# The row maxima brought to the queries by matrix products and copies instead of transfers

## The reference, cut to what matters

```python
# self (units 0 to 15)
scores = where(tril == 0, NEG, where(key_mask == 0, NEG, relu(x@Wq+bq) @ relu(x@Wk+bk).T / sqrt(8)))
out = softmax(scores) * query_mask @ relu(x@Wv+bv) + x ; x = LN(x + gamma * norm(out) + beta)
# ctx (units 16 to 31): 64 rows of another sequence are the keys and values
x = LN(x + softmax(q @ k.T) @ v)
# ffn (units 32 to 47), then experts chosen for each token: the two best of 8
x = x + softmax(causal(q @ k.T)) @ v @ wo + bo
x = x + sum over the 2 best experts of  gate * ffn_e(LN(x))
# ffn (units 48 to 63), then experts chosen for each sequence; LN at the end
```

## Time and profile before

| | us |
|---|---|
| median of 3 runs | 1480.73 (1480.18 to 1484.06) |
| the profiled execution's own time | 1489.51 |
| its span, first to last instruction | 1487.7 |
| PE, DVE, ACT, POOL busy | 1226.8, 949.5, 721.2, 667.1 |
| idle of PE before L714 and L706 until a transfer of the maxima | 54.5 and 10.5 |

### The profile page before, as it was taken

The page is one execution under the profiler, slowest core; times in us unless marked ns, Lnnn a source line. Parts: engine busy times, 40 slices in busy tenths (PEclk is TensorE's granted clock), DMA queues, the critical chain, the costliest instruction groups (busy, mean ns, idle before and its releaser), DMA issues. The chain is left out here.

```text
span 1487.7 us, 29555 instructions
## 1 busy us (share of the span) xinstructions
PE 1226.8 (82%) x9414; PEld 980.7 (66%) x9414; DVE 949.5 (64%) x2854; ACT 721.2 (48%) x1527; POOL 667.1 (45%) x1151
## 2 busy tenths in 40 slices
PE   0598889998898679999997299993788989967998
PEld 0476667775665457777776289982566666746997
DVE  6478799997667688888873201112788787623554
ACT  0165566664444346555653155551355555544543
POOL 2244445464222137777776200003576676432655
PEclk9899999997658789999997589996699999987999
DMA  2676776433555445454521277873555555305774
GB/s 49 178 202 197 207 206 182 118 88 112 149 152 154 127 119 135 127 141 122 135 76 35 61 203 216 222 198 86 159 144 148 138 138 142 99 27 163 204 222 141
DMA packets 210607, 212.86 MB, mean 143 GB/s; under 512 B 46868, under 2 KB 163092, under 8 KB 210453
## 3 DMA queue, kind: packets, MB, share of 16 engines
q1 hardware_dynamic: 193572, 189.59, 47.4%
q10 hardware_dynamic: 12784, 12.98, 2.8%
q0 software_dynamic: 4096, 8.40, 2.0%
HBM read 121.84 MB, written 84.41 MB: 139 GB/s over the span
## 5 line engine op out<-in xcount | busy, mean ns | idle before, releaser
L1215 POOL TENSOR_SCALAR_AFFINE_SELECT probs<-probs 128x256 f32<-128x256 f32 (+1 forms) x576 | 282.1, 495 | 266.2 <-ACT probs L901 261.0
L901 ACT ACTIVATE probs<-weights 128x512 f32<-128x512 f32 x448 | 264.5, 597 | 180.9 <-PE weights L714 142.1
L1061 DVE TENSOR_REDUCE negmax<-scores 128x4 f32<-128x512 f32 x384 | 260.5, 685 | 81.3 <-PE scores L667 78.7
L714 PE MATMUL weights<-queries,keys 104*128 104x256 f32 x768 | 170.5, 307 | 55.0 <-DMA queries<-maxrows 54.5
L714 PEld LDWEIGHTS weights<-queries,keys 104*128 104x128 f32 x768 | 145.5, 205 | 89.6 <-DMA queries<-maxrows 70.5
L667 PE MATMUL scores<-keys,queries 128*128 128x512 f32 (+1 forms) x384 | 192.3, 507 | 8.0 <-DMA queries<-zeros 3.7
L901 ACT ACTIVATE probs<-weights,keybias 128x512 f32<-128x512 f32 x192 | 131.6, 688 | 96.6 <-PE weights L714 77.3
L1065 DVE TENSOR_REDUCE negmax<-scores 128x2 f32<-128x512 f32 (+1 forms) x192 | 129.6, 684 | 42.0 <-PE scores L673 35.1
L1279 POOL DMA_INDIRECT out_room<-expert_rows,y_index x64 | 63.6, 994 | 193.4 <-POOLq L1528 180.8
L719 PEld LDWEIGHTS weights<-queries,keys 104*128 104x128 f32 x768 | 113.9, 196 | 16.5 <-ACT probs L901 6.3
L719 PE MATMUL weights<-queries,keys 104*128 104x128 f32 x768 | 111.4, 269 | 5.0 <-ACT probs L901 4.8
(11 more groups left out here) (257 smaller groups left out, 2662.7 us busy)
## 6 DMA issues: line engine op xcount, KB each, us to landing
windows<-parts SPq DMA_DIRECT2D x192, 192.0 KB
queries<-windows SPq DMA_DIRECT2D x64, 384.0 KB
keys<-windows SPq DMA_DIRECT2D x192, 96.0 KB
hidden_room<-in_m_w SPq DMA_DIRECT2D x71, 256.0 KB, 2.8
out_room<-in_m_w SPq DMA_DIRECT2D x71, 256.0 KB, 3.1
routed_rows<-zeros SPq DMA_DIRECT2D x64, 256.0 KB, 3.2
windows<-parts ACTq DMA_DIRECT2D x64, 120.0 KB
xin<-routed_rows SPq DMA_DIRECT2D x39, 128.0 KB, 3.0
```

What stands on the lines that cost most here:

```text
L714: i = pe.matmul(bank[:, k * T:(k + 1) * T], keys[0:MREND, S4 * a + s, 0:P], queries[0:MREND, s, :], start=True, stop=True)
L901: act.activation(probs[:, n % RING], weight_banks[n % 2][:], ACT.Exp, scale=SCALE, **bias).then_inc(exp_done.sem, 1)
L1061: i = dve.tensor_reduce(most[:, part, s, :], bank[:].rearrange("p (a k) -> p a k", k=P), AX.X, ALU.max, negate=True)
L1215: pool.affine_select(out=block, in_=block, compare_op=ALU.is_ge, fill=0.0, base=0, pattern=[[0, heads], [1, P]], channel_multiplier=-1).th ...
```

## The change

- **Maxima.** `maxparts` keeps its 32 columns at the right end (96 to 127) and zeros ahead of them. A product with the 104 columns from `8*s` on as the stationary side then puts the 8 rows of group s at rows 96 to 103 of the bank. `pe_maxima` does that for two groups in one slot (four products of 128 columns, a full bank) and for the other two in the next. `act_maxima` copies rows 96 to 103 straight into `queries`, one copy of 8 by 512 for each half. The second half's products wait for the first half's copy, and `pe_values_in` for the second's. `maxrows` and `sp_maxrows` are gone.
- **Masks.** `keybias`, `keep` and `keeps` are made by POOL (`pool_masks`), and so is `offset` (`pool_offset`); DVE waits for both.
- **Hiding.** The twelve transfers begin at slot 30, one every 11 or 12 slots.
- **Routing.** `earlier`, `ones` and `route_mask` have the type float32r, that of the kernel's score products, and the two products with `earlier` become one of 16 columns.

```diff
@@ pe_maxima
-            bank.take(pe)
-            for t in range(NT):
-                i = pe.matmul(X[:, t * P:(t + 1) * P], maxparts[g % 2][:, t, :], ident_r[:], start=True, stop=True)
-            i.then_inc(maxT_ready.sem, 1)
-            bank.until(maxrows_taken.sem, maxrows_taken.at(g))
-            yield
+            for half in range(2):
+                bank.take(pe)
+                for k in range(2):
+                    s = 2 * half + k
+                    for t in range(NT):
+                        i = pe.matmul(X[0:MREND, k * T + t * P:k * T + (t + 1) * P], maxparts[g % 2][:, t, 8 * s:8 * s + MREND],
+                                      ident_r[:], start=True, stop=True)
+                i.then_inc(maxT_ready.sem, 1)
+                bank.until(maxrows_placed.sem, maxrows_placed.at(g, half + 1))
+                yield
@@ pe_attend
-            pe.wait_ge(maxrows_placed.sem(g), maxrows_placed.at(g))
+            pe.wait_ge(maxrows_placed.sem, maxrows_placed.at(g, NT))
@@ act_maxima
-            act.wait_ge(maxT_ready.sem, maxT_ready.at(g))
-            if g >= 2:
-                act.wait_ge(maxrows_placed.sem(g - 2), maxrows_placed.at(g - 2))
-            act.copy(M8[g % 2][:], maxima_bank(g).tensor[0:S4 * 8, 0:T]).then_inc(maxrows_taken.sem, 1)
-            yield
+            X = maxima_bank(g).tensor
+            act.wait_ge(stacked.sem(g), stacked.at(g))
+            for half in range(2):
+                act.wait_ge(maxT_ready.sem, maxT_ready.at(g, half + 1))
+                act.copy(Q[g % LANES][MROW:MREND, 2 * half:2 * half + 2, :],
+                         X[MROW:MREND, :].rearrange("p (s t) -> p s t", s=2)).then_inc(maxrows_placed.sem, 1)
+                yield
@@ sp_hiding
-            yield from rest(60)
+            yield from rest(30)
...
+                    yield from rest(11)
...
-                    yield from rest(3)
+                    yield from rest(11)
@@ pe_route
-            pe.matmul(X[:, 0:E], earlier[:], mask[:, 0], start=True, stop=True)
-            pe.matmul(X[:, E:2 * E], earlier[:], mask[:, 1], start=True, stop=False)
-            pe.matmul(X[:, E:2 * E], ones[:], mask[:, 0], start=False, stop=True)
+            pe.matmul(X[:, 0:2 * E], earlier[:], mask[:].rearrange("p t e -> p (t e)"), start=True, stop=True)
+            pe.matmul(X[:, E:2 * E], ones[:], mask[:, 0], start=False, stop=True, skip_group_check=True)
@@ new, on POOL at slots prepare+1 and outputs+3 of a self unit
+        def pool_masks(pool, g):
...
+            pool.wait_ge(gone_ready.sem, gone_ready.at(g))
...
+            pool.tensor_scalar(keybias[:, seq], gone[:], -BIG, None, ALU.mult)
+            pool.tensor_scalar(keep2[g % 2][:], gone[:, :, None].to_broadcast([P, NT, 2]), -1.0, 1.0, ALU.mult, ALU.add)
+            pool.tensor_scalar(keeps[:, seq], gone[:], -1.0, 1.0, ALU.mult, ALU.add).then_inc(masks_ready.sem, 1)
+        def pool_offset(pool, g):
+            pool.wait_ge(resid_loaded.sem(g), resid_loaded.at(g))
...
+            pool.tensor_tensor(offset[:], resid[g % LANES][:], w["a_beta"][:, None, :].to_broadcast([P, NT, C]),
+                               ALU.add).then_inc(offset_ready.sem, 1)
```

54 lines of the change are left out of this document (26 added, 28 removed).

## The result

| kernel | median us (lowest to highest, runs) | ratio to before, 95% interval |
|---|---|---|
| before | 1482.39 (1480.18 to 1485.59, 4) | |
| after | 1443.34 (1437.15 to 1445.59, 4) | 0.970 [0.966, 0.974] |

The account below looks back on a forecast made before the run. DVE's chain to `tok`, late together with the maxima's transfer, was taken to bound self and ffn units. Terms -7 (self), -9.8, -5, +7 (ctx), -7 (passage), 0 (ffn), -0.6 gave -22.4 us: median 1480.73 to 1458, 8 in 10 within 1436 to 1474.

Parts of the forecast that it names:

- The ffn units: Steady ffn units stay at 17.1 and 16.6 us, with a new PE wait of 0.5 to 1.2 at the transposes.
- The first rival: In ffn the removed waits pay in full: units 0.65 and 0.25 us shorter, 13 us, time 1445; chance 0.12.
- ffn: nothing in 28 steady units: Term of the sum for ffn: its 28 steady units gain 0 us, because `tok` comes late too.
- What sets the pace: Self and ffn: DVE's chain to `tok`, which ends 0.05 to 0.06 us before PE's transposes start, sets the pace.
- The self unit: Ordinary self units go from 17.5 to 16.8 or 16.9 us, bound next by PE: -7 in 10 units.
- units 4 and 5: Two self units with hiding transfers ahead of the maxima, 21.40 and 22.00 us, become ordinary: -9.8.
- Unit 0: First self unit: its 5.62 us wait goes, with no `tok` or score late behind it: -5.
- ctx: About nine ctx units at half clock pay 1.0 us, seven at full 0.5, less transfer waits: +7.
- The passage: From ctx to ffn: -7 us for the wait of 4.81 and some of the slow clock behind it.
- The half step: Second half's products wait for ACT's copy: stall of 0.4 us per ffn unit, 0.1 per self unit; bounds 0 and 1.6.
- the slower rival: ACT's late copy stalls PE 1.6 us instead of 0.4 in each unit, deciding from about 1.0: 1511; chance 0.07.
- The shared ports: Rival: work moved to POOL comes back as blocked DVE work, losing 6 us of the gain: 1464; chance 0.15.

Follow-up runs that it names:

- y_transpose: The kernel after, with PE's transposes of `tok` and ACT's copies of them one slot later: 1408.1 us, 0.949 of before.
- b_transpose: The kernel before, transfer kept, with PE's transposes of `tok` and ACT's copies of them one slot later: 1470.2 us, 0.986 of before.
- x_products: The kernel before with each of its two maxima products issued four times, transfer and its wait kept: 1485.2 us, 1.002 of before.
- w_wait: The kernel after with an unused transfer of four small pieces that attention's first product waits for: 1469.2 us, 0.991 of before.
- d_products: The kernel after with each of its eight maxima products issued twice: 1485.3 us, 1.001 of before.
- e_maxima: The kernel before with only the maxima's new products and copies in place of the transfer: 1453.8 us, 0.979 of before.
- y_half: The kernel after with the second half of the maxima one slot later, and the values products too: 1426.1 us, 0.963 of before.

## Why the prediction was right, and where it was off

*The ffn units* were forecast unchanged with a new wait of 0.5 to 1.2 us at the transposes; they are, to 0.01 and 0.08 us, with waits of 0.42 and 0.69 and the rest of the old wait in the half step. The first rival, that the waits pay in full, is ruled out by the units and by `y_transpose`. Yet the stages fell by 9.5 and 7.3 us. The step of the sum that failed is "*ffn: nothing in 28 steady units*": I had priced the unit at full clock and not looked at how many units of before weren't ordinary. The trace of before would have shown six.

*What sets the pace.* The prediction read the delay at `tok` as DVE's own chain setting the length of the units. That is only a part of it. In `y_transpose` and `b_transpose` DVE's work is left as it is and only PE's transposes move, and ffn units go from 17.15 to 16.23 and self units from 17.53 to 16.46. What held the units, as the rows read, was a loop through both engines: PE waited for `tok` with its next scores behind it, and DVE's next reductions need these scores. The change left that loop alone in ffn, so the forecast of the units held, but DVE's or POOL's work was not the only way to shorten it.

*The self unit*: 16.8 to 16.9 was forecast, it is 16.48. The product costs 0.085 and not 0.10, the stall is below 0.1, and the small gaps are 0.17 in all (16.31 busy of 16.48). With units 4 and 5, which gave -10.4 for -9.8, this is -3.

*Unit 0* gave -4.6 for -5. But unit 1 took 21.05 at a clock of 0.74 instead of 17.23, and unit 15 27.0 at 0.66 instead of 22.9; before had unit 0 at 0.63 and unit 15 at 0.83. Half-clock stretches of the start and of the stage's end come at another place, and 9 us of the self gain went there. No term stood for it. In `x_products`, `w_wait` and `d_products` unit 15 is long too (26.9, 26.6, 27.2), in `e_maxima` not (23.8), and the cause stays open.

*ctx*: +7 forecast, -3.9 measured. The unit's prices held: at full clock 7.89 for 7.27, at half about 11.2 for 10.18. What failed is the count of nine units at half clock carried over from a draw of before with a clock of 0.70 in ctx. Three kernels whose ctx code is that of before (masks, hiding, routing) took 134.0, 136.9 and 139.6 at 0.78 to 0.80. With the new maxima it took 131.7 to 145.0, over seven kernels. The products cost there, as 150.7 and 159.7 for the two kernels with idle products show, but whether the change itself costs or gains in ctx stays open.

*The passage* gave -4.6 for -7. *The half step* stalls 0.60, 0.43 and 0.08 us in ffn and self, for 0.4 and 0.1; the slower rival needed 1.0 in each unit and is ruled out. It cost the whole up to 17 us all the same, by `y_half`.

*The shared ports.* POOL's three mask steps took 0.23, 0.20 and 0.20 us and `offset` 0.76; DVE's busy time in a self unit fell from 16.32 to 14.92, more than the 1.05 that the forecast took from it:

```profile
204.19 0.23 POOL L1230 TENSOR_SCALAR keybias<-gone 128x2 f32<-128x2 f32 x1 [0.36 <-DVE gone L1008]
204.38 0.20 POOL L1231 TENSOR_SCALAR keep<-gone 128x4 f32<-128x4 f32 x1
204.53 0.20 POOL L1232 TENSOR_SCALAR keeps<-gone 128x2 f32<-128x2 f32 x1
```

The rest is the two small masks and DVE's two steps `normed<-normed,rstd_post,offset`, which took 0.98 us together at 202.45 in the unit of the earlier trace rows and take 0.60 at 204.62 in unit 8 of after. In sum no work came back as blocked work, so this rival's time was wrong; its mechanism is seen all the same, in the other direction. DVE's `keybias` was itself the blocked step, 0.64 beside POOL's work and 0.17 apart from it in `e_maxima`. The Trainium skill, "SBUF — State Buffer", section "Who interferes with whom", lists DVE's `tensor_scalar` among those that can take the shared pair, when their operands meet its conditions, and says that the second to come blocks for the whole of the other's instruction. The trace agrees: `keybias` starts 0.02 us behind POOL's instruction of 201.14 and ends 0.02 behind it. For `tok` in ffn no run here took POOL's work away, and its 1.05 us stays argued.

*Of the sum*: in the profiles -44 us, for -22.4. The 22 missing are units 33 to 61 with the experts' (-21), ctx (-11) and the ordinary self units (-3), less units 1 and 13 to 15 (+9), the passage (+2) and small ones. Single executions of before lie up to 20 us apart, so that some of ctx's share is chance; the medians have -39.

## What to carry to other kernels

Before you price a wait, look at the next instruction in the same row: if its input arrives just as the wait ends, two events are late together, and moving one of them gives nothing or a part. Then look for the place where an in-order engine stands before something that isn't ready, and try it a slot later; that was worth 35 us in the kernel after, nearly as much as the whole change, and 15 in the kernel before. And price a stage by all its units, not by the ordinary one: list those that fell out of the clock or the rhythm, since a change can bring them back or add some.

## What the runs showed of the hardware

- A float32r product of 104 weight columns and 128 streamed ones starts 0.085 us behind the last; routing's float32r products of 8 streamed columns start 0.11 apart (L807 at 626.05, L808 at 626.16), and the five float32 ones that they replace took 1.04 together.
- ACT's copy of 8 x 512 from PSUM takes 0.58 us, as long as one of 128 x 512.
- POOL takes 0.20 to 0.23 us for a `tensor_scalar` on two to four columns, though 0.71 for its `tensor_tensor` with `rstd` of two columns.
- DVE's `keybias`, a `tensor_scalar` of two columns, takes 0.17 us with POOL idle and 0.64 when it starts 0.02 us behind a POOL instruction of 0.64.
- In nine kernels with eight or more maxima products a unit, 9 of 243 ffn units fell to half clock for a part; in five with two, 39 of 135. Of all 378, the 34 with a single wait of PE of over 1.35 us had 23 of these falls, and the 227 with none of 0.8 us had 3.
